# Attention with transposed probabilities as the stationary operand and row sums from a ones column, in a fused cross-attention and feed-forward kernel

## The reference, cut to what matters

```python
q = (layernorm(x) @ W_tgt.T + b_tgt) * mask            # 8 heads of 16
k, v = split((ctx @ W_src.T + b_src) * mask)           # 8 heads of 16 each
scores = einsum('bthd,bshd->bhts', q, k) / sqrt(16)    # masked keys: -inf
update = einsum('bhts,bshd->bthd', softmax(scores), v) # 128 per token
x = x + concat([layernorm(x), update]) @ W_out.T + b_out
z = quant4(layernorm(x))                               # blocks of 16, a scale and eight magnitudes
h = silu(z @ quant4(w_gate).T) * (z @ quant4(w_up).T)  # 352 wide
out = x + quant4(h) @ quant4(w_down).T
```

## Time and profile before

| | before |
|---|---|
| median of 3 timed runs | 225.11 us (224.66 to 225.33) |
| the profiled execution | 227.31 us, its span 225.5 us |
| TensorE busy | 189.2 us (84% of the span) |
| VectorE busy | 175.6 us (78%) |
| GpSimd busy | 139.5 us (62%) |
| ScalarE busy | 132.9 us (59%) |
| mean granted clock | 0.968 |

### The profile page before, as it was taken

One profiled execution on the slowest core, in us unless ns is written; L12 is line 12 of the kernel. 1 busy time (PEld: TensorE's weight loads), 2 busy tenths in 40 slices (PEclk: granted clock), 3 DMA queues, 4 the chain that ended last, 5 costly groups with the idle time before them and its releaser, 6 DMA issues.

```text
span 225.5 us, 5688 instructions
## 1 busy us (share of the span) xinstructions
PE 189.2 (84%) x2045; PEld 140.5 (62%) x2045; DVE 175.6 (78%) x391; ACT 132.9 (59%) x264; POOL 139.5 (62%) x203
## 2 busy tenths in 40 slices
PE   0779899699699999999999947688898998989454
PEld 0255759549459586684977714466586676767443
DVE  7356977839977979767699869799989889898641
ACT  2366979559468778787777433155365555555421
POOL 5288372635799764819455868975758575755820
PEclk9999999889979999999999996699999999999999
DMA  6999832102000000000000000000110101011011
GB/s 202 309 310 271 281 91 88 58 3 93 3 0 4 3 0 4 3 3 0 3 4 0 4 0 0 0 0 3 49 45 2 47 3 47 0 48 44 7 47 47
DMA packets 13665, 11.97 MB, mean 53 GB/s; under 512 B 766, under 2 KB 10558, under 8 KB 13630
## 3 DMA queue, kind: packets, MB, share of 16 engines
q1 hardware_dynamic: 13078, 11.29, 16.1%
q10 hardware_dynamic: 560, 0.33, 0.5%
HBM read 9.52 MB, written 2.10 MB: 52 GB/s over the span
## 4 chain that ended last, share of the span: by engine, by line
POOL 31%; PE 25%; issue 21%; DVE 10%; ACT 5%; DMA 4%; POOLq 1%; SPq 1%; DVEq 0%; ACTq 0%
POOL wq_y L358 9%; POOL hq L373 8%; PE bank L881 5%; PE bank L869 4%; POOL xn L254 4%; DMA b_out<-in_bo 4%; POOL xq_all L288 2%; DVE st L571 2%; POOL rs L244 2%; PE bank L875 2%; PE bank L949 2%; PE bank L832 2%; ACT val L419 2%; DVE den L608 2%; DVE x_all L626 1%
## 5 line engine op out<-in xcount | busy, mean ns | idle before, releaser
L373 POOL TENSOR_TENSOR hq<-wq_u,sch 128x704 f32<-128x704 f32 x16 | 22.6, 1411 | 20.8 <-DVE wq_u L754 20.8
L937 PE MATMUL bank<-guT,xqT 128*128 128x352 f32 x64 | 25.8, 486 | 3.2 <-DVE hh L727 3.2
L541 ACT COPY hT<-bank 128x384 f32<-128x384 f32 x32 | 15.3, 479 | 22.1 <-PE bank L949 22.1
L961 PE MATMUL bank<-wdT,hT 128*128 128x128 f32 x192 | 26.8, 276 | 1.3 <-ACT hT L541 0.8
L949 PE MATMUL bank<-ident,hq 128*128 128x128 f32 x96 | 16.9, 287 | 12.9 <-POOL hq L373 12.9
L949 PEld LDWEIGHTS bank<-ident,hq 128*128 128x128 f32 x96 | 11.8, 145 | 22.0 <-POOL hq L373 18.2
L940 PE MATMUL bank<-guT,xqT 128*128 128x352 f32 x64 | 25.5, 481 | 0.0
L961 PEld LDWEIGHTS bank<-wdT,hT 128*128 128x128 f32 x192 | 24.0, 192 | 1.9 <-ACT hT L541 1.1
L869 PE MATMUL bank<-cT,wsT 128*128 128x512 f32 x32 | 19.4, 740 | 6.3 <-DMA cT<-in_ctxT 6.3
L358 POOL TENSOR_TENSOR wq_y<-hh,ivh 128x704 f32<-128x704 f32 x16 | 22.2, 1389 | 3.5 <-DVE ivh L742 2.0
L473 ACT ACTIVATE mask_bc<-bank 128x352 f32<-128x352 f32 x32 | 14.7, 460 | 13.6 <-PE bank L937 13.4
(11 more groups left out here) (117 smaller groups left out, 493.6 us busy)
## 6 DMA issues: line engine op xcount, KB each, us to landing
cT<-in_ctxT SPq DMA_DIRECT2D x8, 512.0 KB, 5.9
x_all<-in_x SPq DMA_DIRECT2D x8, 256.0 KB, 5.9
mask_bc<-in_mask_rows SPq DMA_DIRECT2D x8, 256.0 KB, 6.5
out_y<-mask_bc SPq DMA_DIRECT2D x8, 256.0 KB, 2.2
wsT<-in_WsT ACTq DMA_DIRECT2D x1, 256.0 KB, 4.0
w_all<-in_wg SPq DMA_DIRECT2D x1, 176.0 KB
w_all<-in_wu SPq DMA_DIRECT2D x1, 176.0 KB
w_all<-in_wd SPq DMA_DIRECT2D x1, 176.0 KB
```

Source lines behind the costliest of these rows:

```text
L373: nc.gpsimd.tensor_tensor(hq[i][:, :, 0:I].rearrange("p t (n k) -> p t n k", k=BLK), rh[i][:, :, :].rearrange("p (t n) k -> p t n k", t=2) ...
L541: nc.scalar.copy(hT[n % 2][:, :, :].rearrange("p c t -> p (c t)"), t_bank[place % 2][:, 0:IP]).then_inc(t_ok, 1)
L937: nc.tensor.matmul(gu_bank[2 * n % 3][:, 0:I], xqT[g % 2][:, t], guT[:, 0, :], start=True, stop=True).then_inc(pe_g, 1)
L961: last = nc.tensor.matmul(d_bank[:, j * P:(j + 1) * P], hT[n % 2][:, c, :], wdT[:, c, :], start=(c == 0), stop=(c == 2))
```

## The change

`attend` swaps its operands. The transposed probabilities of a head pair (64 tokens of one batch) are stationary, and the 34 columns of the pair in `val` are moving, so that the result is token by channel. `val` gets a 17th column per head (`VW = HD + 1`) that holds ones, written once by four memsets, so that column 16 of each head in the result is that head's row sum. The result of a group (4 tiles x 8 heads x 17) no longer fits one bank: it takes the two banks 4 and 5 (`ao_pair`, which are the former `av_bank` and `o_bank`), and banks 0 and 1 for the last group. `attend` therefore waits for `x2_add` of the group before, which reads `o_bank`.

`row_sum`, `reciprocals`, `expand_reciprocals`, `spread_reciprocals` and `av_evac` are gone. `update` (VectorE) now inverts the 32 sums in PSUM and multiplies the attended values by them, into `upd`, token by channel. It stands ahead of `row_max` in the step. `update_transpose` (TensorE) transposes `upd` behind `k_project`, and `updT_evac` (ScalarE) copies the result to `updT`, between `k_evac(g1, 0)` and the first `exp`.

```diff
+VW = HD + 1
 BLK = 16
...
-        val = [sb(f"val{s}", [P, TILES, 2, PAIRS, 2 * HD]) for s in range(2)]
+        val = [sb(f"val{s}", [P, TILES, 2, PAIRS, 2 * VW]) for s in range(2)]
         mx = [sb(f"mx{p}", [P, TILES, 2], BF16) for p in range(PAIRS)]
         prob = [[sb(f"prob{s}{p}", [P, TILES, 2 * S]) for p in range(PAIRS)] for s in range(2)]
         probT = [sb(f"probT{p}", [P, TILES, P]) for p in range(PAIRS)]
-        den = sb("den", [P, TILES, PAIRS, 2])
-        rden = sb("rden", [P, TILES, PAIRS, 2])
-        rden_bc = sb("rden_bc", [P, TILES, D])
-        updU = sb("updU", [P, GT])
+        rden = sb("rden", [P, TILES, H])
+        upd = sb("upd", [P, TILES, D])
         updT = sb("updT", [P, GT])
...
         a_pair = ctx.enter_context(nc.psum_tensor("a_pair", [P, 2, 512], F32))
-        bank = {i: ctx.enter_context(nc.psum_tensor(f"bank{i}", [P, 512], F32)) for i in (0, 1, 4, 5, 6, 7)}
-        banks = [a_pair[:, i - 2, :] if i in (2, 3) else bank[i] for i in range(8)]
+        s_pair, ao_pair = (ctx.enter_context(nc.psum_tensor(n, [P, 2, 512], F32)) for n in ("s_pair", "ao_pair"))
+        bank = {i: ctx.enter_context(nc.psum_tensor(f"bank{i}", [P, 512], F32)) for i in (6, 7)}
+        pairs = {0: s_pair, 2: a_pair, 4: ao_pair}
+        banks = [pairs[i - i % 2][:, i % 2, :] if i < 6 else bank[i] for i in range(8)]
         s_bank, av_bank, o_bank, w0, w1 = banks[0:4], banks[4], banks[5], banks[6], banks[7]
         gu_bank, ah, d_bank, t_bank = (w0, w1, av_bank), a_pair[:, :, 0:I], o_bank, banks[0:2]
-        last_av = banks[1]
+        attended = [(ao_pair if g < NG - 1 else s_pair)[:, :, :].rearrange("p c (t n) -> p (c t) n", t=2)[
+            :, :, 0:H * VW].rearrange("p t (h n) -> p t h n", n=VW) for g in range(NG)]
+        uT_bank = [av_bank if g < NG - 1 else o_bank for g in range(NG)]
         ld_x = [sem(f"ld_x{g}") for g in range(NG)]
...
                 xs = x_all[:, tiles(g), :]
                 nc.gpsimd.tensor_tensor(xs, xs, b_out[:, :, :].to_broadcast([P, TILES, D]), ALU.add).then_inc(xb_ok, 1)
-            def expand_reciprocals(g):
-                pool.wait_ge(rd_ok, g + 1)
-                past(pool, pe_rd, g)
-                nc.gpsimd.tensor_copy(rden_bc[:, :, :].rearrange("r j (h d) -> r (j h) d", d=HD),
-                                      rden[:, :, :, :].rearrange("r j p e -> r (j p e)").unsqueeze(2).to_broadcast(
-                                          [P, TILES * H, HD])).then_inc(rb_ok, 1)
-
...
             add_bias(0)
             def attn_step(k):
-                g1, g3, g4, g5 = k, k - 2, k - 3, k - 4
-                if on(g3):
-                    expand_reciprocals(g3)
+                g1, g4, g5 = k, k - 3, k - 4
                 if on(g4):
...
                 attn_step(k)
-            expand_reciprocals(NG - 1)
             rstd2_of(NG - 2)
             xn2_of(NG - 2)
...
                 s = g % 2
                 act.wait_ge(pe_v, g + 1)
                 past(act, pe_av, g - 1)
-                act.wait_ge(v_zero, 2)
+                act.wait_ge(v_ones, 4)
                 vp = w0[:, :].rearrange("r (t p e d) -> r t p e d", t=TILES, p=PAIRS, e=2)
                 for b in range(2):
                     for e in range(2):
-                        last = nc.scalar.copy(val[s][64 * e:64 * e + 64, :, b, :, HD * e:HD * (e + 1)],
+                        last = nc.scalar.copy(val[s][64 * e:64 * e + 64, :, b, :, VW * e:VW * e + HD],
                                               vp[64 * b:64 * b + 64, :, :, e, :])
                 last.then_inc(v_ok, 1)
-            def av_evac(g):
-                act.wait_ge(pe_av, g + 1)
-                past(act, updT_ok, g)
-                nc.scalar.copy(updU[:, :], (av_bank if g < NG - 1 else last_av)[:, :]).then_inc(av_ok, 1)
+            def updT_evac(g):
+                act.wait_ge(pe_uT, g + 1)
+                past(act, pe_o, g)
+                nc.scalar.copy(updT[:, :], uT_bank[g][:, :]).then_inc(updT_ok, 1)
             def xnT_evac(g):
                 act.wait_ge(pe_xnT, g + 1)
                 n = g * PAIRS + p
                 act.wait_ge(pe_mm, n + 1)
                 past(act, pe_T, n + 1 - 2 * PAIRS)
-                past(act, sum_ok, n + 1 - 2 * PAIRS)
                 nc.scalar.activation(prob[g % 2][p][:, :, :].rearrange("p j c -> p (j c)"), s_bank[p][:, :], ACT.Exp,
                                      scale=float(HD) ** -0.5).then_inc(p_ok, 1)
...
                     normalise1(g1)
-                if on(g3):
-                    av_evac(g3)
                 if on(g1) and k > 0:
                     xnT_evac(g1)
                     k_evac(g1, 0)
                 if k == NG:
                     x0_evac()
+                if on(g3):
+                    updT_evac(g3)
                 if on(g2):
                     exp(g2, 0)
                     exp(g2, 1)
             for m in range(NT + LAG + 1):
                 if m < NT:
                     silu(m)
-                if m == 0:
-                    av_evac(NG - 1)
+                if m == 1:
+                    updT_evac(NG - 1)
                 if m % TILES == 1 and on(m // TILES + 1):
                     xqT_evac(m // TILES + 1)
...
-            def row_sum(g, p):
-                dve.wait_ge(p_ok, g * PAIRS + p + 1)
-                past(dve, rd_ok, g)
-                nc.vector.tensor_reduce(den[:, :, p, :], prob[g % 2][p][:, :, :].rearrange("r j (e s) -> r j e s", e=2),
-                                        AX.X, ALU.add).then_inc(sum_ok, 1)
-
-            def reciprocals(g):
-                dve.wait_ge(sum_ok, (g + 1) * PAIRS)
-                past(dve, rb_ok, g)
-                nc.vector.reciprocal(rden[:, :, :, :], den[:, :, :, :]).then_inc(rd_ok, 1)
-
             def update(g):
-                dve.wait_ge(av_ok, g + 1)
-                dve.wait_ge(pe_rd, g + 1)
-                past(dve, pe_o, g)
-                nc.vector.tensor_tensor(updT[:, :], o_bank[:, :], updU[:, :], ALU.mult).then_inc(updT_ok, 1)
+                dve.wait_ge(pe_av, g + 1)
+                nc.vector.reciprocal(rden[:, :, :], attended[g][:, :, :, HD]).then_inc(rd_ok, 1)
+                dve.wait_ge(rd_ok, g + 1)
+                past(dve, pe_uT, g)
+                nc.vector.tensor_tensor(upd[:, :, :].rearrange("p t (h d) -> p t h d", d=HD), attended[g][:, :, :, 0:HD],
+                                        rden[:, :, :].unsqueeze(3).to_broadcast([P, TILES, H, HD]),
+                                        ALU.mult).then_inc(upd_ok, 1)
             def x2_add(g):
                 dve.wait_ge(pe_o, g + 1)
...
             stats1(1)
+            dve.wait_ge(v_zero, 2)
+            for s in range(2):
+                for e in range(2):
+                    nc.vector.memset(val[s][64 * e:64 * e + 64, :, :, :, e * VW + HD], 1.0).then_inc(v_ones, 1)
             def attn_step(k):
                 g1, g2, g3, g4 = k, k - 1, k - 2, k - 3
                 if on(g4):
                     x2_add(g4)
                     stats2(g4)
+                if on(g3):
+                    update(g3)
                 if on(g2):
                     for p in range(PAIRS):
                         row_max(g2, p)
-                if on(g3):
-                    update(g3)
                 if on(g4):
                     block_max(g4)
                 if on(g1):
                     dve.wait_ge(ld_o, 32)
                     nc.vector.tensor_tensor(b_out[:, 0, :], o_bank[:, 0:D], b_out[:, 0, :], ALU.add).then_inc(bo_ok, 1)
                     stats1(2)
-                if on(g2):
-                    for p in range(PAIRS):
-                        row_sum(g2, p)
-                        if p == 0 and on(g4):
-                            block_reciprocal(g4)
-                    reciprocals(g2)
-                elif on(g4):
+                if on(g4):
                     block_reciprocal(g4)
                 if on(g1 + 3):
...
                 pe.wait_ge(v_ok, g + 1)
-                past(pe, av_ok, g)
+                past(pe, updT_ok, g)
+                past(pe, x2_ok, g)
                 past(pe, w_sb, min(g - 3, 3))
-                bank = av_bank if g < NG - 1 else last_av
-                for j in range(TILES):
-                    for b in range(2):
-                        for p in range(PAIRS):
-                            last = nc.tensor.matmul(bank[32 * p:32 * p + 32, j * P + b * S:j * P + (b + 1) * S],
-                                                    val[g % 2][:, j, b, p, :], probT[p][:, j, b * S:(b + 1) * S],
-                                                    start=True, stop=True)
+                pe.wait_ge(bo_ok, 1)
+                for j in range(TILES):
+                    for p in range(PAIRS):
+                        for b in range(2):
+                            last = nc.tensor.matmul(
+                                attended[g][64 * b:64 * b + 64, j, 2 * p:2 * p + 2, :].rearrange("r h n -> r (h n)"),
```

(28 more changed lines are left out.)

12 lines of the change are left out of this document (6 added, 6 removed).

## The result

| | before | changed |
|---|---|---|
| median of the timed runs | 225.22 us (4 runs, 224.66 to 228.19) | 229.06 us (4 runs, 227.56 to 229.68) |
| ratio | | 1.0169 (95% interval 1.010 to 1.0238) |
| the profiled execution, its span | 227.31, 225.5 us | 229.53, 227.7 us |
| TensorE, VectorE busy | 189.2, 175.6 us | 194.6, 158.5 us |

A forecast was written before the change was run, and what follows sets the result against it. TensorE's own queue was taken to bound the attention phase. The terms -0.65 - 0.8 + 1.0 + 1.7 = +1.25 us on the profiled 227.31 gave 228.6, scaled 1% down to 226.3 us; range 223.0 to 230.0.

The forecast's parts named there:

- a drop of the clock in step 5: In TensorE's new wait for `x2_add`: a possible 1.5 us on top of the forecast's worst, allowed for in the range.
- Attend: TensorE's 64 attend matmuls: 1.8 us instead of 1.03, +0.77 per attend, with two column groups loading side by side.
- bound by its stream: Rival for the attend matmuls: weight loads hide, attend takes 1.1 us, time 223.6 us; chance 0.2.
- one after another: Rival for the attend matmuls: loads of the two halves do not overlap, attend takes 3.6 us, time 238; chance 0.1.
- Step 2: Attention step without TensorE idle time: transposes only change place, attend adds 0.77, so +0.8 us.
- Steps 6 and 7: Steady attention steps: four update transposes behind `k_project` cost +0.5 us each, +1.0 together.
- Steps 2 and 3: Attention steps together: -0.65 us, taking 1.4 us of TensorE's stop without the low clock; ends +1.0 and -2.1.
- the second rival: The TensorE stop at attend's end in step 3 vanishes, -2.1 instead of -0.65: 224.9 us; chance 0.2.
- Steps 4 and 5: The wait for `rden_bc` goes (-2.3), a new wait for `x2_add` and longer work come (+1.5): -0.8 us together.
- Step 8: Last attention step and handover: maxima wait behind attend and `update`, `x2_add` of group 6 moves from 122.01 to 123.7, +1.7 us.
- VectorE: Engine freed of 32 row sums, 19.8 us: predicted about 20 us less busy.
- The sum: All step terms added: +1.25 us on the profiled 227.31 us, 228.6, put 1% lower at 226.3 us.

The follow-up runs named there:

- The new order of step 8: Changed kernel with step 8's row maxima ahead of `update`, and the update's transpose and copy moved later; ratio 1.0126 to the kernel before.
- the second profile: The kernel before, unchanged, timed against itself and profiled again; ratio 1.0008, span 227.1 us.

## Why the prediction was right, and where it was short

Slower was forecast, by 1.1 us to 226.3, and the measured 229.06 lies in the range of 223 to 230, near its end. Direction and mechanism held; the size did not. The change cost 3.8 us, more than three times the 1.1 forecast, and 229.06 lies outside the forecast's own range of 225 to 228.5. That it is inside the wide one is partly luck: that range was stretched for an attend of 2.3 us or a drop of the clock in step 5, and neither happened. Step by step, against the profile on which it was made:

- *Attend:* 1.8 us predicted, 2.0 measured. The two ends were 1.1 and 3.6, and the value taken was the right one of the three for the right reason, shown by three kernels: the load of 64 columns sets it (half the columns, about half the time; twice the stream, 0.05 us), one half alone takes 50 to 59 ns a matmul, as priced, and two halves run side by side. The rivals "bound by its stream" and "one after another" fell. That two groups halve the time was an assumption that came true, and not shown by the rows behind it: by the same price four groups brought 1.8 us down to 1.03, not to a quarter. In the experiments two halves with 32 columns are as fast (16 ns) as the four quarters of the kernel before; what holds the quarters back stays open. The Trainium skill ("TensorE: Matmul & The Clock Gate", Part 3, "The mechanism") lets a load overlap matmuls in flight only across row groups. All these loads use all 128 rows, and yet two alternating halves start a matmul every 31 ns where one half alone needs 50 to 59: the measurement decides against the rule.
- *Step 2:* +0.8 predicted, +0.9 measured. *Steps 6 and 7:* +1.0 predicted, +0.95 measured, by the transposes behind `k_project`, with the longer attend under the wait for `normalise1`.
- *Steps 2 and 3:* -0.65 predicted, -1.4 measured (+0.9 and -2.3). The -0.65 was a value near the middle of its two ends and no sum of terms. The stop shrank to 0.3 us and the clock stayed up, nearly the second rival (chance 0.2). I had taken 0.4 us off the stop for the slower attend; over all profiles it is 1.1 to 1.8 us at the fast pace and at most 0.7 at the slow one.
- *Steps 4 and 5:* the 1.9 us wait and the low clock went and a wait for `x2_add` came, as predicted, but in both steps: step 4 took 14.5, not 13.9 us. TensorE reached it 1.5 us earlier than I had assumed and `x2_add` only 0.9 (55.3 instead of 56.2): I had not carried the gain of step 3 into step 4, where it met this wait. -0.2 measured, -0.8 predicted.
- *Step 8:* the chain was the predicted one. `x2_add` of group 6 moved by 1.9 us against its step's start, 1.7 predicted; the step grew by 2.25 us. The new order of step 8 took 1.45 of it back.
- *VectorE:* 17 us less busy, not 20. The 19.8 of the earlier trace rows adds up instructions that overlap at their ends: without the sums and 2.8 us of reciprocals the kernel before was 20.2 us less busy.
- *The sum:* these steps make +1.7 us and the span grew by 2.2; the rest is in the feed-forward phase, where one more drop of the clock fell near its end. Against its own profile the prediction of +1.25 was 1 us short. The 0.3% that I took for what a measurement can tell was too little: the intervals of the ratios here reach 0.3 to 0.7% to either side.

The step that failed is the last one of the sum: "The timed runs' median is 225.11, 1% below the profiled time; I put the difference on that: 226.3 us". It took the profiled execution for a longer copy of the timed ones. But 2.4 of its microseconds in steps 3 to 5 were a longer stop (0.7) and low clock, absent in the second profile, so most of what I booked as regained there (part of -0.65 and of -2.3) was not there to regain in an ordinary execution. Against the second profile of before (92.6 us for steps 2 to 8) the changed kernel needs 96.7: +0.9 in step 2, +0.1 in step 3, -0.1 in 4 and 5 together, +0.95 in 6 and 7, +2.25 in step 8. That is +4.1, and the two timed comparisons give +2.5 and +3.8. The size of single drops of the clock in timed runs can't be read, so how often an ordinary execution has them in attention stays open; the thirteen other profiles have none there.

What the freed VectorE bought is settled too: without the row sums the kernel before gains 2.5 us, all in step 4. The change had that gain in hand and spent most of it on waits for `x2_add`, which attend had not waited for: 2.1 us in steps 4 and 5, by the late `s3_round`.

## What to carry to other kernels

When one engine's queue is full, work moved off another engine is worth only the waits it ends; count the moved work by where it lands in the full queue, because the same four transposes are free in front of a wait and cost their full time behind it. A buffer that now covers two banks brings a second wait with it: look at what stands in front of the instruction that is waited for, here a rounding that nobody needed yet. And where the profiled execution is longer than the timed ones, find the microseconds that only it has before using its stages as a baseline.

## What the runs showed of the hardware that was not expected

- In pairs of load and float32 matmul over all 128 rows, a load of 64 columns in two alternating halves of the array gives a matmul every 31 ns, with 34 moving columns, and 32 ns with 68. Where one half is at work alone the starts are 50 to 59 ns apart. Eight matmuls in a row to each half give 37 ns on average, not 56, because the other half is taken up before this one is through.
- A load of 32 columns gives a matmul every 16 ns, in two halves with 34 moving columns and in four quarters with 64.
- At 16 ns a matmul TensorE stops in some places with no releaser named: 1.1 to 1.8 us in step 3 in six profiles, 6.1 us in five places with twice as many matmuls; at 31 to 32 ns at most 0.7 us, at 37 ns not at all.
- A stop of 1.1 us and a wait of 1.9 us left the granted clock at 2.4 GHz in one execution (steps 3 and 4 of the second profile), a stop of 1.7 and a wait of 1.6 in another; behind 1.8 and 1.9 us in the same places it fell to 1.2 GHz for 3.4 us each in a third.
